# W1 as three rounded products over 256 moving columns in a quantised residual adapter stack

## What is computed

```python
gi = sum(|x| <= thresholds)                  # 8 groups; idx = min(gi, 7)
q  = where(gi == 8, 0, (clip(round(x / d[idx]) + zp[idx], 0, 63) - zp[idx]) * d[idx])
x1 = x + q
x2 = x1 + x1 @ W1[adapter].T                 # W1: 1024 x 1024 per adapter, one of 8 per sequence
x3 = x2 + x2 @ W2.T + 0.5 * (x2 @ lora_A[label]) @ lora_B.T
out = x3 + (x3 @ B[adapter].T) @ A[adapter].T
```

## Time and profile before

| | us |
|---|---|
| median of 3 runs (lowest, highest) | 486.75 (483.95, 487.24) |
| span of the profiled execution | 481.9 |
| median less that span, taken for what lies around it | 4.85 |
| TensorE busy | 464.9 (96%) |
| VectorE busy | 419.4 (87%) |
| ScalarE busy | 358.6 (74%) |
| GpSimd busy | 45.5 (9%) |

### The profile page before, as it was taken

How to read it: one execution, slowest core, us unless ns; L and a number is a source line. 1 busy time by engine, 2 the same in 40 slices (tenths; PEclk the granted TensorE clock), 3 DMA queues, 4 the chain that set the end, 5 groups by cost and what they waited for, 6 DMA issues and landing times.

```text
span 481.9 us, 8215 instructions
## 1 busy us (share of the span) xinstructions
PE 464.9 (96%) x3184; PEld 424.7 (88%) x3184; DVE 419.4 (87%) x481; ACT 358.6 (74%) x383; POOL 45.5 (9%) x46
## 2 busy tenths in 40 slices
PE   3999869999999999999999999999999999999997
PEld 3969669898999989898999989898999989898995
DVE  5999999999999899989999899989999899989120
ACT  6979958678877879678877879678887879675011
POOL 1064000200002000200002000210003000100000
PEclk9999989999999999999999999999999999999999
DMA  7997214712335122712335122712335122702002
GB/s 282 407 415 258 113 34 149 294 54 97 131 127 212 44 95 97 294 44 103 131 120 218 44 89 101 294 44 103 131 101 237 44 86 104 294 2 88 1 1 87
DMA packets 17830, 67.07 MB, mean 139 GB/s; under 512 B 2576, under 2 KB 5904, under 8 KB 13712
## 3 DMA queue, kind: packets, MB, share of 16 engines
q1 hardware_dynamic: 17808, 66.81, 37.9%
HBM read 56.84 MB, written 9.96 MB: 139 GB/s over the span
## 4 chain that ended last, share of the span: by engine, by line
PE 90%; ACT 3%; DMA 3%; DVE 2%; issue 1%; POOL 1%; SPq 0%; DVEq 0%
PE x_bank L603 45%; PE acc L628 34%; PE acc L579 3%; PE x_bank L616 3%; PE acc L640 2%; PE acc L638 2%; DMA w1b<-w 2%; DMA rows<-own_rows 1%; ACT mask L344 1%; ACT w2h L400 1%; DVE y L460 1%; PE acc L567 1%; ACT tq L329 1%; PE acc L577 0%; ACT outb L404 0%
## 5 line engine op out<-in xcount | busy, mean ns | idle before, releaser
L603 PEld LDWEIGHTS x_bank<-x,w1b 128*128 128x128 f32 x2048 | 233.2, 193 | 8.2 <-issue 4.9
L603 PE MATMUL x_bank<-x,w1b 128*128 128x128 f32 x2048 | 234.8, 276 | 3.7 <-DVE x L475 3.7
L344 ACT ACTIVATE mask<-absx,negtop 128x1024 bf16<-128x1024 f32 x112 | 128.4, 1146 | 40.3 <-DVE y L460 39.5
L329 ACT ACTIVATE tq<-xin,magic,rdelta 128x1024 f32<-128x1024 f32 x128 | 157.0, 1234 | 0.6 <-DVE yhigh L526 0.3
L460 DVE COPY_PREDICATED y<-mask,uq 128x1024 f32<-128x1024 int16 x112 | 151.1, 1349 | 0.1
L439 DVE TENSOR_SCALAR tq<-tq,par 128x1024 f32<-128x1024 f32 x128 | 99.2, 775 | 3.7 <-DVE y L460 3.1
L448 DVE TENSOR_SCALAR uq<-tq,ylow,yhigh 128x1024 f32<-128x1024 f32 x112 | 92.3, 824 | 0.2 <-DVE y L460 0.2
L628 PE MATMUL acc<-w2h,x2h 128*128 128x512 f32 x256 | 80.9, 393 | 2.0 <-DVE x2l L481 2.0
L628 PE MATMUL acc<-w2h,x2l 128*128 128x512 f32 x256 | 79.9, 390 | 0.0
L628 PE MATMUL acc<-w2l,x2h 128*128 128x512 f32 x256 | 79.2, 390 | 0.0
L295 POOL TENSOR_TENSOR w1b<-w1b,eye 128x256 f32<-128x256 f32 x32 | 36.5, 1140 | 368.9 <-DMA w1b<-w 368.9
(11 more groups left out here) (57 smaller groups left out, 218.9 us busy)
## 6 DMA issues: line engine op xcount, KB each, us to landing
w1b<-w SPq DMA_DIRECT2D x32, 1024.0 KB, 6.7
xin<-x SPq DMA_DIRECT2D x16, 512.0 KB, 3.7
out<-outb SPq DMA_DIRECT2D x14, 512.0 KB, 2.8
w1b<-w2n SPq DMA_DIRECT2D x4, 1024.0 KB, 10.6
ring<-w2t SPq DMA_DIRECT2D x6, 512.0 KB, 6.7
ua<-e_dram SPq DMA_DIRECT2D x16, 128.0 KB, 2.5
ua<-w2t SPq DMA_DIRECT2D x2, 512.0 KB, 7.8
va<-la SPq DMA_DIRECT2D x8, 128.0 KB, 2.7
```

The costliest lines, as they stand in the source:

```text
L329: nc.scalar.activation(tq[:, n % TQ, :], flat(xin, c % UN), ACT.Identity, bias=magic[:, 0:1], scale=rdelta[:, g:g + 1]).then_inc(t_ready, 1)
L344: nc.scalar.activation(mask[:, n % MK, :], absx[:, :], ACT.Relu, bias=negtop[:, g:g + 1], scale=1.0).then_inc(mask_ready, 1)
L603: last = nc.tensor.matmul(x2_bank[2 * t + i][:, o % HALF * P:(o % HALF + 1) * P], w1b[:, o, at:at + P], x1[:, t, k, :], start=(o % HALF == ...
```

## The change

- Batch 0 stays as it is, except that w2g no longer lies in w1b's memory, so that W1's first loads wait for nothing.
- **W1 from batch 1 on** is split: w1s holds four items of two output blocks each, with a rounded part (part 0) and a rest (part 1). A half h of W1 covers input features 512 h to 512 h + 511. `round_w1`: a casting DMA, issued by GpSimd, from DRAM to part 0. `negate_w1`: ScalarE writes its negative into part 1. `w1_remainder`: an accumulating DMA, issued by GpSimd, adds W1 to that. Each is 512 KB, and there are eight items per batch.
- **Units** of batch 1 on are 512 features by 256 rows (unit 2b + h), again 128 x 1024 elements and eight steps. `w1_half(b, h)` gives for each of 8 output blocks 3 x 4 products of 256 moving columns, and for the four blocks that lie in the half two with the identity, which replace GpSimd's diagonal: 104 products. It is done for h = 1 at the start of `batch(b)` and for h = 0 of the next batch behind v_x2.
- **x1**: in units 4 to 13 GpSimd issues a DMA that adds ycut to xin (`sum_x1`) and a casting one into x1h (`round_x1`). In units 2, 3, 14 and 15 (DIRECT) VectorE adds and ScalarE rounds. VectorE splits x1l off in all (`split_x1`) at step 8c + 12 (8c + 11 in DIRECT).
- **u** is loaded by casting DMAs (three places of two row ranges each), negated by ScalarE (one operation for two), and completed by two accumulating DMAs; VectorE's `split_u` is gone.
- ycut has memory of its own. x2's banks hold pairs of output blocks for 256 rows; they are rounded at steps 16b + 23 to 26 and split at 16b + 22 to 25.
- At the end, the last batch does the half h = 1 of W1, product(0), v, product(1) and u_low after its last unit. The loops over batches are written out.

The diff, cut to its core:

```diff
+    HC = HALF * P
+    SLOT = (0, 2, 1, 3)
+    DIRECT = (2, 3, UN * B - 2, UN * B - 1)
...
-                sp.wait_ge(g_tiles, 2 * (j + 1))
...
+            def round_w1(b, h, j):
+                m = item(b, h, j)
+                if m < PAIRS:
+                    pool.wait_ge(w1_used, 2 * (j // 2) + 2)
+                else:
+                    pool.wait_ge(item_used, m - PAIRS + 1)
+                nc.gpsimd.dma_start(w1s[:, SLOT[j], 0, :], w1_item(b, h, j)).then_inc(h_in[j], 16)
+
+            def w1_remainder(b, h, j):
+
+                pool.wait_ge(h_negated, item(b, h, j) + 1)
+                nc.gpsimd.dma_start(w1s[:, SLOT[j], 1, :], w1_item(b, h, j).bitcast(f32r), accum_op=ALU.add) \
+                    .then_inc(l_in[j], 16)
+
+            def sum_x1(c):
+                if c < UN * B and c not in DIRECT:
+                    pool.wait_ge(y_cut, c + 1)
+                    nc.gpsimd.dma_start(xin[:, c % UN, :], ycut[:, :], accum_op=ALU.add).then_inc(x1_in, 16)
+
+            def round_x1(c):
+                if c < UN * B and c not in DIRECT:
+                    b, h = divmod(c, UN)
+                    pool.wait_ge(x1_in, 16 * x1_sums(c))
+                    pool.wait_ge(item_used, item(b - 1, h, PAIRS))
+                    nc.gpsimd.dma_start(x1h[:, h, :, :].rearrange("p k t -> p (k t)"), xin[:, h, :]) \
+                        .then_inc(x1h_in[h], 16)
...
+            adapter = {b: pool.value_load(ids_a[0:1, b:b + 1], min_val=0, max_val=NA - 1) for b in (0, 1)}
+            round_u(0)
+            for j in range(PAIRS):
+                round_w1(1, 0, j)
+            w1_remainder(1, 0, 0)
+            w1_remainder(1, 0, 1)
+            w1_remainder(1, 0, 2)
+            w1_remainder(1, 0, 3)
+            u_remainder(0)
+            for c in range(UN, UN * B):
+                b, h = divmod(c, UN)
+                if h:
+                    round_u(b)
+                if c + 1 < UN * B:
+                    nb, nh = divmod(c + 1, UN)
+                    if nh == 0:
+                        adapter[nb] = pool.value_load(ids_a[0:1, nb:nb + 1], min_val=0, max_val=NA - 1)
+                    round_w1(nb, nh, 0)
+                    round_w1(nb, nh, 1)
+                    round_w1(nb, nh, 2)
+                    w1_remainder(nb, nh, 0)
+                    round_w1(nb, nh, 3)
+                    w1_remainder(nb, nh, 1)
+                    sum_x1(c + 1)
+                    w1_remainder(nb, nh, 2)
+                    w1_remainder(nb, nh, 3)
+                    round_x1(c + 1)
+                if h:
+                    u_remainder(b)
...
         ACT_X2, DVE_X2 = (14, 16), (13, 15)
+        ACT_BANK, DVE_BANK = (23, 24, 25, 26), (22, 23, 24, 25)
+        ACT_NEG = (25, 26, 27, 28)
+        ACT_X1, DVE_X1 = 12, (11, 12)
 
         ACT_V, DVE_V = 14, 15
-        ACT_U, DVE_U = 21, 23
-        ACT_LOW, DVE_LOW = 26, 27
-        ACT_OUT = (30, 30, 31, 32)
-        END = STEPS + PER + 1
+        ACT_U = 29
+        ACT_LOW, DVE_LOW = 31, 30
+        ACT_LOW0, DVE_LOW0 = 26, 27
+        ACT_OUT = (35, 35, 39, 39)
+        END = STEPS + 2 * PER
...
+            def negate_w1(b, h, j):
+                m = item(b, h, j)
+                act.wait_ge(h_in[j], 16 * (m // PAIRS + 1))
+                nc.scalar.activation(w1s[:, SLOT[j], 1, :], w1s[:, SLOT[j], 0, :].bitcast(f32), ACT.Copy, scale=-1.0) \
+                    .then_inc(h_negated, 1)
+
+            def round_x1(c):
+                b, h = divmod(c, UN)
+                act.wait_ge(x1_ready, x1_adds(c))
+                if b == 1:
+                    act.wait_ge(w1_used, PAIRS)
+                else:
+                    act.wait_ge(item_used, item(b - 1, h, PAIRS))
+                nc.scalar.activation(x1h[:, h, :, :].rearrange("p k t -> p (k t)"), xin[:, h, :], ACT.Copy) \
+                    .then_inc(x1h_ready[h], 1)
...
+                if c:
+                    dve.wait_ge(x1_ready, x1_adds(c - 1))
+                    if x1_sums(c - 1):
+                        dve.wait_ge(x1_in, 16 * x1_sums(c - 1))
+                nc.vector.scalar_tensor_tensor(ycut[:, :], absx[:, :], top[:, G - 1:G], y[:, :],
                                                ALU.is_gt, ALU.mult).then_inc(y_cut, 1)
                 dve.wait_ge(y_cut, c + 1)
                 if G * (c + 1) < STEPS:
                     clamp(G * (c + 1))
                 if c == 1:
                     dve.wait_ge(g_out, 16)
-                nc.vector.tensor_tensor(flat(x1, c % UN), flat(xin, c % UN), ycut, ALU.add).then_inc(x1_ready, 1)
-
-            def split_x2(c, i):
-                t = c % UN
-                dve.wait_ge(x2h_ready, 2 * c + i + 1)
-                tiles = slice(i * HALF, (i + 1) * HALF)
-                nc.vector.tensor_tensor(x2l[:, t, tiles, :].rearrange("p k t -> p (k t)"), x2_bank[2 * t + i][:, :],
-                                        x2h[:, t, tiles, :].rearrange("p k t -> p (k t)").bitcast(f32),
+                if c < UN:
+                    nc.vector.tensor_tensor(flat(x1, c), xin[:, c, :], ycut[:, :], ALU.add).then_inc(x1_ready, 1)
+                elif c in DIRECT:
+                    nc.vector.tensor_tensor(xin[:, c % UN, :], xin[:, c % UN, :], ycut[:, :], ALU.add) \
+                        .then_inc(x1_ready, 1)
+
+            def split_x1(c):
+                b, h = divmod(c, UN)
+                dve.wait_ge(*x1h_made(c))
+                nc.vector.tensor_tensor(x1l[:, h, :, :].rearrange("p k t -> p (k t)"), xin[:, h, :],
+                                        x1h[:, h, :, :].rearrange("p k t -> p (k t)").bitcast(f32),
+                                        ALU.subtract).then_inc(x1l_ready[h], 1)
...
+                for c in range(UN, UN * B):
+                    if n == G * c + DVE_X1[0 if c in DIRECT else 1]:
+                        split_x1(c)
...
+            def w1_half(b, h):
+
+                pe.wait_ge(*x1h_made(UN * b + h))
+                if b == 1:
+                    pe.wait_ge(eye_ready, 1)
+                for j in range(PAIRS):
+                    pe.wait_ge(l_in[j], 16 * (UN * (b - 1) + h + 1))
+                    if h == 0 and j == 2:
+                        pe.wait_ge(lowl_ready, b)
+                    for o in (2 * j, 2 * j + 1):
+                        into = x2_bank[j][:, o % 2 * T:(o % 2 + 1) * T]
+                        for part, xs in ((0, x1h), (1, x1h), (0, x1l)):
+                            if j == 0 and xs is x1l and o == 0:
+                                pe.wait_ge(x1l_ready[h], b)
+                            for k in range(HALF):
+                                at = o % 2 * HC + ((k - o) % HALF if o // HALF == h else k) * P
+                                last = nc.tensor.matmul(into, w1s[:, SLOT[j], part, at:at + P], xs[:, h, k, :],
+                                                        start=(h == 0 and o % 2 == 0 and part == 0 and xs is x1h
+                                                               and k == 0),
+                                                        stop=False, skip_group_check=True)
+                        if o // HALF == h:
+                            for xs in (x1h, x1l):
+                                last = nc.tensor.matmul(into, eye_r[:, :], xs[:, h, o % HALF, :], start=False,
+                                                        stop=False, skip_group_check=True)
+                    last.then_inc(item_used, 1)
...
+            def batch(b):
+                w1_half(b, 1)
+                for k in range(KT):
+                    if k % 2 == 0:
+                        pe.wait_ge(x2l_ready, BANKS * b + k // 2 + 1)
+                    if k == 0:
+                        pe.wait_ge(out_ready, ACCS * (b - 1) + 2)
+                    product(0, k)
+                pe.wait_ge(vl_ready, 2 * (b + 1))
+                v_x2(b, range(KT))
+                if b < LAST:
+                    w1_half(b + 1, 0)
+                    u_low(b, 0)
+                    u_low(b, 1)
+                pe.wait_ge(out_ready, ACCS * b)
+                if b < LAST:
+                    for k in range(KT):
+                        product(1, k)
+                    u_low(b, 2)
+                    u_low(b, 3)
```

More of the change, by code:

```diff
@@ L117, in quantised_residual_adapter_stack @@
         u_in = sem("u_in")
+        ul_in = sem("ul_in")
+        h_in = [sem(f"h_in{j}") for j in range(PAIRS)]
+        l_in = [sem(f"l_in{j}") for j in range(PAIRS)]
+        x1_in = sem("x1_in")
         v_in = sem("v_in")
@@ L165, in selections, with item, low_bank, x1_adds @@
             return n - n // G
+        def item(b, h, j):
+            return 2 * PAIRS * (b - 1) + PAIRS * h + j
+        def low_bank(b):
+            return x2_bank[3] if b else x2_bank[2]
+        def x1_adds(c):
+            return min(c + 1, UN) + sum(d <= c for d in DIRECT)
+        def x1_sums(c):
+            return c + 1 - x1_adds(c)
+        def x1h_made(c):
+            direct = len([d for d in DIRECT if d <= c and d % UN == c % UN])
```

(24 more changed lines are left out.)

336 lines of the change are left out of this document (181 added, 155 removed).

## The result

The changed kernel takes 611.12 us, median of 4 runs (608.44 to 614.51), the kernel before 486.96 in runs on the same chip (483.95 to 487.24): 1.2587 times as long, with an interval of 1.2532 to 1.2641. The forecast was 517 and at most 550. The profiled execution took 608.44, its span 606.5.

What follows compares the result with a forecast made beforehand. TensorE bounds the kernel, VectorE close behind; after the change, waits decide. Span 93.8 + 3 x 27.3 + 10 x 29.3 + 2.2 + 37.7 + 3.2 = 511.8, with 4.85 added 517 us; range 480 to 550.

Steps and rivals of the forecast that it cites:

- the wait named: VectorE's x1 split in units 4 to 13 waits 4.9 us for the casting DMA that makes x1h.
- the landing at 2.8: x1's 512 KB casting DMA lands in 2.8 us, taken from a store with SBUF as source; bound 2.8 to 6.7.
- the DMA load: Traffic of 13.6 MB per batch, 52 of 58.6 us with accumulated bytes counted twice, hides but lengthens landings.
- L: Time from a unit's cut to x1h being there: 6.4 + 1.8 + 2.8 = 11.0 us, range 9.9 to 17.4.
- The rest of the unit: VectorE's work in units 4 to 13 behind the wait for x1h: 24.4 - 6.1 = 18.3 us.
- The tail: Last cut's end to span's end: 2.2 for cut, addition and rounding, 37.7 with TensorE's work, then 3.2 us.
- The 4.85 us between span and time: Difference of the earlier kernel's median, 486.75, from its profiled span, 481.9, added to the forecast span.
- TensorE's 29 us: Gain over seven batches from TensorE's work alone, its sum per batch going from 54.1 to 49.9 us.
- A: Rival: the cast is there in time and TensorE decides, so faster, 471 us; chance 0.17.
- B: Rival: the wait is half as long, a unit takes 26.3 us, time 487, no change; chance 0.10.
- C: Rival: GpSimd is the bound or starved, issues 2.15 and landing 6.7 us, time 581; chance 0.11.
- The rule against the change: VectorE's two-port modes keep GpSimd from writing DMA descriptors; two issues would cost 5 us more, time 567.

Runs made afterwards that it cites:

- Experiments 3: The changed kernel with GpSimd issuing x1's cast ahead of the accumulating DMAs of W1's third and fourth items: 578.37 us, ratio 1.1876.
- experiment 7: Separate DMA-only kernel: a 512 KB cast alone and behind two plain, casting or accumulating DMAs; two ahead cost 3.3 us, or 5.3 if accumulating.
- experiment 1: The changed kernel without x1's two DMAs per unit, VectorE adding and ScalarE rounding x1 in every unit: 544.45 us, ratio 1.1179.
- 4: The changed kernel without W1's accumulating DMAs, TensorE waiting for the negations instead: 547.37 us, ratio 1.1239.
- 5: The changed kernel with x1's sum and cast both issued right behind the first of W1's four accumulating DMAs: 555.77 us, ratio 1.141.
- 8: experiment 1 with ScalarE's x1 rounding a step earlier, VectorE's bank split a step later and its low-rank split two later: 512.73 us, ratio 1.0526.
- 9: 8 with the low rank one step earlier (ScalarE 30, VectorE 31): 496.05 us, ratio 1.0195.
- experiment 11: 9 without W1's accumulating DMAs, TensorE waiting for the negations instead: 484.6 us, ratio 0.9983.
- 6: Separate DMA-only kernel: single 512 KB transfers, VectorE idle or busy; plain or casting issues 0.53 to 0.69 us idle, 0.55 to 0.94 busy.
- experiment 12: experiment 1 with W1's negations on GpSimd in place of ScalarE: 588.65 us, ratio 1.2085.

## Why the prediction was wrong in size and right in kind

**Right: the bound, and the wait that replaces it.** The prediction says "so what is waited for decides", and the wait named, its ten occurrences and its releaser are what the trace has; its place behind W1's fourth item holds in the units of even number. The clock, too, falls behind the idle times, as was left in the range; since TensorE waits again before the next half, it should add little to the unit, but it was not tried apart. A rounded product of 256 columns takes 0.12 us at full clock (twelve in 1.44), forecast 0.1175; ScalarE's chain 6.35 for 6.4; GpSimd's issue for the cast 0.55 to 0.9 for 0.9. TensorE's work after the last x1 is 38.0 (565.35 to 603.38) for 37.7. What GpSimd's issues cost VectorE was put at nothing, and it is nothing: VectorE's clamp takes 826 ns in the mean where it took 824, its value 759 where it took 775.

**The step that failed: the landing at 2.8.** "I take 2.8, the row with the same source" and, on the DMA load, "It hides, but lengthens landings". The load itself was well estimated: 52 us of 58.6 per batch; the windows from 152.7 to 526.2 give a share of 0.77, that is 57.5 us in the 74.7 that a batch now takes. But a share below one hides only what nobody waits for. The cast stands in one queue behind accumulating DMAs, at the moment of full load (1.02). Experiments 3 and 7 show both prices: 2.9 with none ahead, 6.2 to 8.2 behind two. The other end of the bound, 6.7 "among others in flight", was the nearer one, in part by luck: the prediction calls it a landing of 512 KB, but the row is of W1 loads of 1024 KB in another queue. No row before the change had the same neighbours. Even with 6.7 the prediction's own sum gives L = 14.9 and 223.7 + 10 x 33.2 = 556, so the landing alone isn't all of the error.

**The wait that was not seen: the sum.** The chain counted ScalarE alone. The cast also needs the sum to have landed, 7.9 us behind its issue. In units of odd number this decides (x1h at 17.6 to 20.1 behind the cut). Together with the landing it makes L 16.4 in place of 11.0, 54 us. Timed unit by unit, the cast lands 7.1 behind its issue in the mean in place of 2.8, which makes 43 us; in the five units of odd number it is issued 4.2 us later than in the others, 21 us, of which 14.1 are the wait for the sum; and the two issues, 0.8 in place of 1.8 ahead of the landing, give 10 back. Taken away from either side the loss is of that order: 67 us less without the DMAs on the path (experiment 1), 64 less without the accumulating ones of W1 (4), 55 by order alone (5).

**The rest of the unit, 20.9 in place of 18.3.** VectorE's 18.3 was made of busy times. Three of its steps need what ScalarE does one step later (rounded x1 in DIRECT units, rounded banks, low rank). In the kernel without x1's DMAs, moving them costs no work and brings 32 us (8) and 17 more (9). Unit 3, 32.4 for 27.3, goes the same way: 32.1 from cut to cut in experiment 1, 27.6 in 8. That the order costs the changed kernel its 26 us is likely. In its ten units alone (VectorE's waits from 152 to 527) the two that are left come to 25.3:

```profile
DVE x2l L633 <- ACT x2h L462: 14.8, 15, 1.3
DVE low_lh L645 <- ACT low_lh L501: 10.5, 5, 2.1
```

It was not tried there alone, though, and the first of the two stood before the change as well, 35.5 over the whole run.

**The tail, 50.6 in place of 43.1.** The half of W1 was reckoned to start when x1 is there. The chain of the changed kernel shows TensorE still at the batch before:

```profile
553.52 10.91 PE acc L808 x48
565.35 7.19 PE x_bank L782 x60
```

VectorE splits x1 at 558.28; TensorE takes W1 up at 565.35, behind product(1). The forecast start was 2.2 behind the cut's end, 558.1: these 7.2 us are nearly the whole 7.5. 9 us were said to be given back at the end. By cuts it is more: from the last cut's start to the end of the span the kernel before needs 36.7 us (445.24 to 481.9), experiment 11 53.0 (429.81 to 482.8). At its last cut experiment 11 is 15.4 us ahead of the kernel before, and these 16 us are why even this version, with part of the DMAs left out, only equals it.

**The 4.85 us between span and time.** The sum adds them as what lies around the span, but only about 2 do: single runs have 487.17 for a span of 485.4 and 608.44 for 606.5. The profiled span of before, 481.9, therefore belongs to the fastest run, 483.95, and not to the median. The profiled run was the fastest after the change as well (611.12 less 606.5 is 4.62), so this error cancelled by luck.

**Where TensorE's 29 us went.** With hardly anything late a unit takes 26.0 (11), against 27.2 before, and not TensorE's forecast 25.0: all three engines have some 25.5 us to do in it, TensorE too. Over ten units that is 12 us of gain. 16 us go at the end. The accumulating DMAs cost 11.5 more (9 against 11). The steps' order and x1's DMAs make the other 115.

**The rivals.** A needs the cast in time; that never happened, and with nearly every wait gone (11) the time is 484.6, not 471: a unit takes 26.0, not 25, with all three engines full, and the tail is longer. B is what the cleaned version (9) comes near to, by another way. C's time, 581, is the nearest of all, but not for its reason: GpSimd is busy 26%, and an issue takes 0.68 or 0.94 in the mean for W1 and 1.3 at most for the sum, where C wanted 2.15; only its landing of 6.7 was near.

**The rule against the change.** In these runs a GpSimd issue is not starved: beside a VectorE without a gap it takes at most 1.03 us (6). In the changed kernel W1's take 0.68 and 0.94 in the mean (the longest 1.75), the sum's up to 1.3. The Trainium skill, SBUF — State Buffer, section "SBUF: two separate sides", gives 620 ns for a DMA issued by GpSimd alone and some 3100 beside a VectorE copy. The first is near the 0.53 to 0.69 us that plain and casting issues took with VectorE idle. The second no run here shows: the measurement decides for the operations tried, float32 of 1024 columns; a plain VectorE copy was not among them. What does hold is that a computing GpSimd slows VectorE (12).

## What to carry to other kernels

Take a DMA's landing time from a row with the same neighbours in its queue, not from one with the same shape: order in the queue moved this one from 2.9 to 7.0 us, though the DMA engines' mean share was only 0.77. Where engines are balanced to a few per cent, lay the steps of all their programs side by side before counting busy time, and put no consumer ahead of its producer (32 us, experiment 1 against 8) and neither of them too late for the engine that comes next (17 us, 8 against 9). And when work is shifted towards the end of a pipeline, cost the drain from the last input to the last output, with what the engine still has in hand by then.

## What was not expected of the hardware

- A casting DMA of 512 KB is no dearer than a plain one (3.8 both, from DRAM), an accumulating one takes 5.6 from DRAM and 4.5 from on-chip memory, against 3.8 and 3.0.
- GpSimd's issue behind an accumulating one takes 1.23 us in place of 0.55 (experiment 7, the cast behind two accumulating).
- After 8.4 us of idling TensorE ran its first eight products at 0.234 us each, the 1.2 GHz level, the next four at 0.215, and from 320.3 on eight in 0.95, 0.12 each.
- A 1024-column negation takes GpSimd 3.2 us beside a working VectorE (experiment 12), ScalarE 1.05.
